# A two-layer interaction kernel whose first pair products are made and summed at other places in the opening

## The reference

```
for k in 0, 1, 2:
    z = einsum('bmd,bhd->bdmh', x, prev)        # prev = x at k = 0
    t = z.reshape(b, d, m*h) @ w[k] + bias[k]
    t = t / sqrt(sum over (unit, d) of t*t)     # one norm per example
    prev = t
logit = sum over d of all t                      # 3 * 128 features
h = relu([logit, dense_ctx] @ W_top1 + b_top1); h = relu(h @ W_top2 + b_top2); y = h @ W_top3
```

## Time and profile before

| | us |
|---|---|
| median of 3 runs | 1047.56 (1046.0 to 1047.68) |
| the profiled execution's own time | 1048.04 |
| its span | 1046.3 |
| PE busy | 1018.3 (97%) |
| DVE busy | 967.4 (92%) |
| POOL busy | 872.2 (83%) |
| ACT busy | 795.4 (76%) |

### The profile page before, as it was taken

One profiled execution on the slowest core, in us unless ns is written; L12 is line 12 of the kernel. 1 busy time (PEld: TensorE's weight loads), 2 busy tenths in 40 slices (PEclk: granted clock), 3 DMA queues, 4 the chain that ended last, 5 costly groups with the idle time before them and its releaser, 6 DMA issues.

```text
span 1046.3 us, 17971 instructions
## 1 busy us (share of the span) xinstructions
PE 1018.3 (97%) x4320; PEld 786.6 (75%) x4320; DVE 967.4 (92%) x3345; ACT 795.4 (76%) x2655; POOL 872.2 (83%) x729
## 2 busy tenths in 40 slices
PE   2999999999999999999999999999999999999998
PEld 0477877878787787877778787777878777787883
DVE  2599999999999999999999999999999999999993
ACT  3476878878787887878788787878878787888872
POOL 6878989898888989888898989889898887777770
PEclk9999999999999999999999999999999999999999
DMA  5550030412103030210303021030302103000000
GB/s 186 134 150 9 6 87 3 99 51 64 29 7 86 3 90 3 57 36 5 87 3 90 3 57 36 5 88 3 91 2 53 40 5 88 1 1 1 2 1 1
DMA packets 75892, 46.10 MB, mean 44 GB/s; under 512 B 55689, under 2 KB 58633, under 8 KB 75658
## 3 DMA queue, kind: packets, MB, share of 16 engines
q1 hardware_dynamic: 68938, 39.33, 15.7%
q0 software_dynamic: 5120, 1.29, 1.3%
q10 hardware_dynamic: 1728, 4.33, 1.1%
HBM read 42.99 MB, written 1.94 MB: 43 GB/s over the span
## 4 chain that ended last, share of the span: by engine, by line
PE 93%; DVE 4%; POOL 1%; issue 1%; DMA 1%; ACT 0%; SPq 0%; DVEq 0%; ACTq 0%
PE bank_d L734 14%; PE bank_d L736 13%; PE bank_d L735 13%; PE bank_a L734 13%; PE bank_a L736 13%; PE bank_a L735 13%; PE acc L794 8%; DVE sums L962 2%; PE turned L777 1%; PE turned L815 1%; POOL gathered L433 1%; PE bank_d L889 1%; PE bank_a L844 1%; PE small L803 0%; DMA base_sb<-in_bases 0%
## 5 line engine op out<-in xcount | busy, mean ns | idle before, releaser
L450 POOL TENSOR_TENSOR sums<-sums,scaled 128x512 f32<-128x512 f32 (+1 forms) x512 | 660.2, 1290 | 112.7 <-ACT scaled L576 79.3
L962 DVE SCALAR_TENSOR_TENSOR sums<-bank_d,x_col,sums 128x128 f32<-128x128 f32 x2304 | 656.8, 339 | 30.3 <-PE bank_d L736 21.5
L576 ACT ACTIVATE scaled<-bank_a,x_col 128x128 f32<-128x128 f32 x1920 | 555.8, 385 | 133.5 <-PE bank_a L736 125.0
L734 PE MATMUL bank_d<-w_hi,prev_lo 128*128 128x512 f32 x640 | 279.0, 436 | 2.3 <-DVE sums L981 2.0
L734 PE MATMUL bank_a<-w_hi,prev_lo 128*128 128x512 f32 (+1 forms) x640 | 269.5, 421 | 2.3 <-issue 1.6
L736 PE MATMUL bank_d<-w_hi,prev_hi 128*128 128x512 f32 x640 | 252.6, 395 | 0.0
L735 PE MATMUL bank_d<-w_lo,prev_hi 128*128 128x512 f32 x640 | 252.4, 394 | 0.0
L736 PE MATMUL bank_a<-w_hi,prev_hi 128*128 128x512 f32 (+1 forms) x640 | 245.3, 383 | 0.0
L735 PE MATMUL bank_a<-w_lo,prev_hi 128*128 128x512 f32 (+1 forms) x640 | 244.9, 383 | 0.0
L576 ACT ACTIVATE sums<-bank_a,x_col 128x128 f32<-128x128 f32 x512 | 146.6, 370 | 65.3 <-PE bank_a L736 64.4
L433 POOL DMA_INDIRECT gathered<-in_table,idx x160 | 169.0, 1056 | 28.3 <-issue 14.8
(11 more groups left out here) (85 smaller groups left out, 536.3 us busy)
## 6 DMA issues: line engine op xcount, KB each, us to landing
x_pairs<-x_scratch SPq DMA_DIRECT2D x138, 156.0 KB
x_pairs<-x_scratch SPq DMA_DIRECT2D x99, 78.0 KB
gathered<-in_table,idx POOLq DMA_INDIRECT x160
x_sq<-x_scratch SPq DMA_DIRECT2D x32, 64.0 KB
x_pairs<-x_scratch SPq DMA_DIRECT2D x93, 22.0 KB
x_scratch<-gathered SPq DMA_DIRECT2D x16, 72.0 KB
w_raw<-in_w ACTq DMA_DIRECT2D x1, 1024.0 KB, 4.8
w_raw<-in_w ACTq DMA_DIRECT2D x1, 896.0 KB
```

Of the source, the lines that this page charges most:

```text
L450: nc.gpsimd.tensor_tensor(out=sums[:, n % SUMS, 0:w, :], in0=sums[:, n % SUMS, 0:w, :], in1=scaled[:, a - 1, 0:w, :], op=ALU.add).then_inc ...
L576: op = nc.scalar.activation(to[:, i, :], bank_a[at % A_RING][:, i * UNITS:(i + 1) * UNITS], ACT.Copy, scale=x_of(c, q, a * PER_BANK + i))
L734: nc.tensor.matmul(to, lo, w_h, start=True, stop=False)
L962: nc.vector.scalar_tensor_tensor(out=taken(n, u) if u in LEFT else total, in0=taken(n, u), scalar=x_of(c, q, A_FIELDS + u), in1=total, op0 ...
```

## The change

The main parts, with all that is edited:

```
+LEAD_TILES = {5: 0, 6: 1}
 for _c in range(1, CHUNKS):
     _it = _c - 1
     if _it == 0:
-        _made = []
-        _summed = {(0, 0): [0, 1], (0, 2): [2, 3], (0, 4): [4, 5], (0, 6): [6]}
+        _made = [None, None, (0, 3), (0, 7)]
+        _summed = {(0, 0): [2], (0, 1): [3], (0, 3): [4], (0, 4): [5], (0, 6): [6]}
...
-    PAIRS_AT.update({at: (_c, p) for p, at in enumerate(_made)})
+    PAIRS_AT.update({at: (_c, p) for p, at in enumerate(_made) if at})
...
-GATHERS_BEFORE = 7
+GATHERS_BEFORE = 6
...
             for at in range(LEAD):
                 bank_for_act(at)
+                if at in LEAD_TILES:
+                    pair_matmul(1, LEAD_TILES[at])
...
                 make_pairs(0, p)
+            sum_squares(0, 0)
             turn_x(0)
-            for piece in range(W2_FIRST):
-                split_low(2, piece)
-            sum_squares(0, 0)
             for step in range(R_STEPS):
                 reciprocal_step(0, step)
...
             features(0)
-            for p in range(NP):
+            for piece in range(W2_FIRST):
+                split_low(2, piece)
+            for p in range(2):
                 make_pairs(1, p)
```

## The result

| | before | changed |
|---|---|---|
| median of 20 runs each, us | 1046.36 (1045.21 to 1047.68) | 1048.22 (1046.86 to 1049.25) |
| ratio | | 1.0016, 95% interval 1.0009 to 1.0023 |
| the profiled execution's own time, us | 1048.04 | 1048.33 |
| its span, us | 1046.3 | 1046.6 |

The changed kernel is slower by 0.16%, 1.7 us (0.9 to 2.4), inside the 0.2% that were called "no change that can be told" and on the side that was forecast. That the forecast time, 1048.3, meets the measured median is partly luck: the three runs and the profile that were shown of before lay high (the profiled 1048.04 is above all of the 20 runs).

A forecast was written before the change was run, and what follows sets the result against it. PE's gapless row in the opening, then ACT and DVE, was taken to set the time. Splits, turn, p = 2 and 3 and gathers 0, tiles +0.77 us: 1047.56 + 0.77 = 1048.3 us, range 1046.9 to 1049.6.

The forecast's parts named there:

- no change that can be told: Whole kernel: the forecast outcome, a difference within about 0.2% (2.1 us), on the slow side; chance 0.94.
- What bounds the kernel: Opening: PE's gapless work from 47.87 to 60.16, then ACT, `sum_squares` and DVE to 88.25; PE waits there pass on fully.
- The splits: DVE behind `features`, from 43.61: 2.09 us hidden by the wait for chunk 1's rows until 46.75; cost 0.
- the turn: `turn_x(0)` on DVE, now behind chunk 0's `sum_squares`: 0.45 us fits in 0.73 us of idleness; cost 0.
- p = 2 and p = 3: Chunk 1's products on DVE: fields of step 0 fill p = 2's 0.45 us wait; both count 0.
- the gather at 0: POOL: one 1.06 us gather moved from ahead of the first add into step 0; cost 0.
- the second rival: Adds of step 0: POOL and the splits collide, delaying p = 1's product; +2.1 us, 1049.7; chance 0.10, past 53.8 0.04.
- the first rival: Opening: DVE's freed time counts, saving 0.45 us before p = 2 and 0.72 before `sum_squares`; 1.17 us, 1046.4; chance 0.12.
- The third rival: Opening: the loss is absorbed by quieter DVE instructions beside POOL or earlier chunk 1 rows; neutral, 1047.6; chance 0.16.
- The product tiles: PE among lead banks and step 0: new idleness before tiles 0 (0.53) and 2 (0.24), 0.77 us lost.
- The sum is set by tile 2 alone, so a faster p = 0 wouldn't help: PE's opening: tile 2, waiting for p = 1's product, starts at 52.54 instead of 51.77, fixing the whole 0.77 us.

The follow-up runs named there:

- e0: The kernel before again, without any edit, for a second profile and the scatter; ratio 1.0001 (0.9992 to 1.0010).
- e1: The changed kernel with its product tiles summed by PE where they were before, all else staying changed; 0.9996 (0.9987 to 1.0005) against before.
- e2: The kernel before with only the product tiles moved on PE, DVE's and POOL's orders as before; 1.0007 (0.9998 to 1.0016), median 1047.64 us against 1046.61.
- e7a: The changed kernel with three more dummy matmuls of 0.86 us on PE ahead of the lead banks; 1.0018 (1.0009 to 1.0027) against before.
- e7b: The kernel before with three more dummy matmuls of 0.86 us on PE ahead of the lead banks; 1.0018 (1.0009 to 1.0027) against before.
- v1: The changed kernel with no product tile among the lead banks and the tiles later than before; 1.0002 (0.9990 to 1.0015) against before.
- v2: The kernel before with ACT's squares of chunk 1 ahead of bank 10's scaling instead of behind it; 0.9991 (0.9976 to 1.0007) against before.
- e6: The changed kernel with chunk 1's products p = 0 and 1 made from chunk 0's rows, loads not waiting for chunk 1's store; 1.0010 (1.0001 to 1.0019) against before.
- e3: The changed kernel with tiles 0 and 1 left among the lead banks, tiles 2 and 3 back at place 2 of step 0; 1.0012 (1.0003 to 1.0021).
- e4: The changed kernel with tiles 0 and 1 behind lead banks 3 and 4 instead of 5 and 6; 1.0037 (1.0024 to 1.0049), median 1050.67 us.
- e5: The changed kernel with seven gathers of chunk 2 ahead of POOL's adds again, as before; 1.0023 (1.0011 to 1.0034) against before.

## Why the prediction was right, and where its size was off

**What bounds the kernel: right.** From `sum_squares` to the product of chunk 2 it is 26.13 us in both, and PE's row of work from lead bank 5 to bank 10 was where it was decided: 12.98 us against 11.58. That row takes 11.57 to 11.62 us in every other profile at full clock in which PE doesn't wait in it (e0, e1, e2, e7a, e7b, v1). e7b shows that what delays PE ahead of it is passed on. The times named for `sum_squares` (62.9) and chunk 2's first tile (90.5) came to 62.45 and 90.01, because the whole lead began 0.67 us earlier in this execution.

**The splits, the turn, p = 2 and p = 3, the gather at 0: right.** e1 has them all and runs at 0.9996. Their collision with POOL's adds, the second rival, did not reach the product tiles: the splits took 2.09 us as before, the adds of step 0 6.40 us against 6.09, and the product of p = 1 1.39 against 1.33.

**DVE's freed time counts, the first rival: refuted by the profile.** In e1 DVE idles for it elsewhere, and the yardstick is that of e0 (45.14 and 45.13); e1's time alone (0.9987 to 1.0005) would still leave room for it. The third rival, that the loss is absorbed, is outside the interval of the result. Its premise, that the 0.72 us before `sum_squares` is on the path, was not refuted: v2 frees it from the other side, by ACT, and the stretch behind gets shorter by 0.8 us. DVE's freed time goes nowhere because PE and ACT set that moment, as the prediction had it.

**The product tiles: the right step, mis-sized.** The idleness before tiles 0 and 2 was put at 0.53 + 0.24 = 0.77 us. In the changed kernel's profile the row of work grew by 1.40 us, some 1.2 of it at tile 0 (1.01 us of shown wait, and a slower start behind it) and 0.2 at tile 2; the runs give 1.7 (0.9 to 2.4). The sum itself was sound. With the changed kernel's own times it gives 51.96 + 0.15 - (46.81 + 3.90) = 1.40 us, which is what was measured; with e6's, 51.58 + 0.15 - (47.57 + 3.90) = 0.26, where its row grew by 0.27; with e7a's (52.57 and 49.59) it gives no wait, and there was none. What was off is the two times that went into it, lead bank 5 at 47.87 (A) and the end of the product of p = 1 at 52.39 (B), both from one execution. The same sum from the other profiles whose opening is the same up to there gives 1.35 (e0: 52.10 and 47.00), 0.39 (e1: 51.87 and 47.73), 1.43 (e3: 52.44 and 47.26) and 1.42 (v1: 52.63 and 47.46), and nothing in e2. So 0.77 was one draw out of 0 to 1.4. The range of the sum should have taken in an earlier A, and took in only another B. That the forecast size lies just below the interval, and not further off, is as much a matter of that draw as of the working.

**"The sum is set by tile 2 alone, so a faster p = 0 wouldn't help": not tested by itself.** For the new order as it stands the sums above bear it out, since tile 2's product alone gives the 1.40 us. But it would mislead whoever takes tile 2's wait away: most of the 1.40 us stands before tile 0, and e3, with no early tile 2, is still at 1.0012 with 0.98 us of wait. Either tile is enough for most of the loss.

**Not foreseen:** that such a wait can take the clock down. In the changed kernel 1 of 20 runs had a mean clock under 1.00, in e3 2 of 11, in e4 5 of 6, and of the kernel before's 61 runs in the first two groups none, nor any of e2, e6, e7a and e7b (11 each). On the third chip it fell without any tile in the lead (v2), so such a wait is one way to it and not the only one. For the changed kernel itself it adds little.

**Open:** whether more than scatter keeps e6 at 1.0010 with nearly all of PE's wait gone; whether the 1.7 us of the runs hold more than the up to 1.4 us that the profiles account for; why e2 lies 1.0 us above its kernel before by the medians and the changed kernel 1.9 (the intervals of the two overlap).

## What to carry to other kernels

Work that is moved up in a queue is moved towards its inputs: before moving it, look at what lands last for it, and count everything that stands behind it. Where the slack is the difference of two chains that move against each other, one profile gives one draw of it; take it from several executions, or delay one chain on purpose by dummy work, as e7a and e7b did. If a filler for an engine's pauses waits on a transfer, it makes a pause of its own.

## What the runs showed of the hardware

The granted clock of TensorE fell from 1.00 to 0.50 (2.4 to 1.2 GHz) inside the opening, behind the lead banks with their pauses and one wait of 0.98 us (e3), where it did not fall in the changed kernel's profile behind a wait of 1.01 us, nor in e4's profiled run behind one of 1.83 us. So with pauses like these it differed from one execution to the next. The rows at either level: a bank's matmuls started 0.43 us apart (51.33 to 51.76, e3) against 0.23. The runs with it lay about 2 us above their kernel's others in e3 (1050.0 against 1047.7).

The Trainium skill, TensorE: Matmul & The Clock Gate, Part 1, says that the gate has just the two levels of 1.2 and 2.4 GHz. The stretches of e3 agree: 0.50 where the fall filled a stretch, and 0.82 and 0.83 in those that it covered in part.

On one chip ACT stopped among the lead banks for up to 2.97 us with no releaser in the profile (e5). The kernel before had no profile there; 9 of its 34 runs had a mean clock below 1.00, and none of 61 on the two others, so it seems to have been disturbed too. Differences of 0.1% could not be told there.
